# First cross-attention: the next unit's scores are moved ahead of this unit's transposes on TensorE, and its maxima ahead of the copies on VectorE

## The reference

```python
q = (x @ Wq).reshape(B, Nq, 16, 64)      # 112 rows
k = (context @ Wk).reshape(B, Nk, 16, 64)  # 375 rows
v = (context @ Wv).reshape(B, Nk, 16, 64)
scores = einsum('bqhd,bkhd->bhqk', q, k) / 8
attn = softmax(scores, axis=-1)
out = einsum('bhqk,bkhd->bqhd', attn, v).reshape(B, Nq, 1024) @ Wo + bo
x = layernorm(x + out)
```

## Time and profile before

| | |
|---|---|
| three timed runs | 1081.72 us median, 1080.94 to 1088.02 |
| the profiled execution | 1089.54 us, of which the span of instructions is 1087.7 us |
| TensorE busy | 1000.9 us, 92% |
| VectorE busy | 584.4 us, 54% |
| ScalarE busy | 411.1 us, 38% |
| mean granted TensorE clock | 0.964 of 2.4 GHz |
| first scores to last weigh of the first cross-attention | 143 to 465 us of the span |

### The profile page before, as it was taken

How to read it: one execution, slowest core, us unless ns; L and a number is a source line. 1 busy time by engine, 2 the same in 40 slices (tenths; PEclk the granted TensorE clock), 3 DMA queues, 4 the chain that set the end, 5 groups by cost and what they waited for, 6 DMA issues and landing times. The chain is left out here.

```text
span 1087.7 us, 17961 instructions
## 1 busy us (share of the span) xinstructions
PE 1000.9 (92%) x6656; PEld 775.4 (71%) x6656; DVE 584.4 (54%) x1316; ACT 411.1 (38%) x1068; POOL 150.5 (14%) x151
## 2 busy tenths in 40 slices
PE   6899799999999999969999996888889999999985
PEld 4587677877877877659999995565566767676653
DVE  1877545546555555646565554457524443544543
ACT  2555534333343343324545341366523222322221
POOL 0233410010110100004434342100010000000000
PEclk9999899999999999879999997999989999999996
DMA  4500000000000000046112000600000000001000
GB/s 147 187 2 1 30 15 2 15 15 2 14 0 0 0 0 0 1 171 191 40 39 77 0 2 29 136 2 2 2 18 15 15 15 15 15 1 27 5 5 13
DMA packets 24286, 34.34 MB, mean 32 GB/s; under 512 B 3168, under 2 KB 19888, under 8 KB 24224
## 3 DMA queue, kind: packets, MB, share of 16 engines
q1 hardware_dynamic: 24224, 33.51, 10.3%
HBM read 30.75 MB, written 2.75 MB: 31 GB/s over the span
## 5 line engine op out<-in xcount | busy, mean ns | idle before, releaser
L1041 ACT ACTIVATE x_prob<-bank,x_negmax 112x375 f32<-112x375 f32 x128 | 72.3, 570 | 154.7 <-DVE x_negmax L957 154.7
L1684 DVE TENSOR_TENSOR moe_h_low<-moe_sq,moe_h_high 128x448 fp32r<-128x448 f32 x64 | 54.7, 873 | 52.9 <-ACT moe_h_high L1749 39.6
L1725 POOL TENSOR_TENSOR moe_sq<-moe_r 128x448 f32<-128x448 f32 x64 | 64.1, 1004 | 122.8 <-ACT moe_r L1757 104.3
L88 PE MATMUL bank<-moe_w_low,moe_h_high 128*112 128x256 f32 x256 | 71.8, 280 | 0.0
L88 PE MATMUL bank<-moe_w_high,moe_h_high 128*112 128x256 f32 x256 | 71.7, 280 | 0.0
L88 PE MATMUL bank<-moe_w_high,moe_h_low 128*112 128x256 f32 x256 | 71.7, 280 | 0.0
L957 DVE TENSOR_REDUCE x_negmax<-bank 112x1 f32<-112x375 f32 x128 | 64.1, 543 | 8.4 <-PE bank L849 6.4
L1757 ACT ACTIVATE moe_r<-bank 128x448 f32<-128x448 f32 x64 | 34.9, 546 | 86.8 <-PE bank L88 85.1
L1436 ACT ACTIVATE x_prob<-bank,x_negmax 112x375 f32<-112x375 f32 x64 | 36.1, 569 | 75.9 <-DVE x_negmax L1306 75.9
L870 PEld LDWEIGHTS bank<-x_prob_t,x_v 125*64 125x64 f32 x768 | 38.1, 139 | 34.5 <-issue 30.5
L962 DVE COPY x_prob_t<-bank 125x336 f32<-125x336 f32 x128 | 58.9, 499 | 5.7 <-PE bank L858 3.7
(11 more groups left out here) (368 smaller groups left out, 2281.6 us busy)
## 6 DMA issues: line engine op xcount, KB each, us to landing
moe_w<-in_L_ffn_W SPq DMA_DIRECT2D x16, 512.0 KB, 4.6
ctx_t<-in_ctx_t SPq DMA_DIRECT2D x8, 376.0 KB, 4.4
x_ctx_t<-in_ctx_t SPq DMA_DIRECT2D x8, 376.0 KB, 3.3
wk<-in_L_xattn_Wk SPq DMA_DIRECT2D x2, 1024.0 KB, 6.9
wv<-in_L_xattn_Wv SPq DMA_DIRECT2D x2, 1024.0 KB, 9.7
wq<-in_L_xattn_Wq SPq DMA_DIRECT2D x2, 1024.0 KB, 11.8
wo<-in_L_xattn_Wo SPq DMA_DIRECT2D x2, 1024.0 KB, 13.3
w_in<-in_L_attn_W_in SPq DMA_DIRECT2D x1, 1160.0 KB, 7.2
```

The costliest lines, as they stand in the source:

```text
L88: last = pe.matmul(out, lhs, rhs, start=(k == 0), stop=(k == len(pairs) - 1))
L1041: act.activation(PROB(u, e)[:, :], S_BANK(u, e)[0:T, 0:S], ACT.Exp, bias=negmax[:, g:g + 1], accum_out=total[:, g:g + 1]).then_inc(p_ready, 1)
L1684: dve.tensor_tensor(h_low[half][:, m, :], sq[m % 2][:, :], h_high[half][:, m, :].bitcast(F32), ALU.subtract).then_inc(low_done, 1)
L1725: pool.tensor_tensor(sq[m % 2][:, :], r[m % 2][:, :], r[m % 2][:, :], ALU.mult).then_inc(sq_done, 1)
```

## The change

The code order of two calls is swapped on TensorE and on VectorE, and two waits are added. On TensorE a unit is now scores(u + 1), turn(u), weigh(u - 1), jobs. On VectorE it is row_max(u + 1), copy_turned(u), emptying. Each score now waits by itself for the exponential that reads its bank (`p_ready` of the same head of the unit before). Each exponential now waits until the transposes of the unit before have read its buffer (`pt_ready`), since they no longer stand ahead of the scores that it needs. No instruction is added or taken out but the waits, and the register arithmetic that they need in the loop.

```diff
@@ TensorE, scores
                     for e in range(PER):
                         rows = slice(e * DH, (e + 1) * DH)
+                        wait_past(pe, p_ready, (i * U + u - 1) * PER + e + 1)
                         last = pe.matmul(S_BANK(u, e)[0:T, 0:S], qt[p][rows, u, :], kt[p][rows, u, :], start=True, stop=True)
@@ TensorE, round_
                         if heads:
-                            turn(i, u)
                             if u + 1 < U:
                                 scores(i, u + 1, p)
                             elif front:
                                 scores(i + 1, 0, 1 - p)
+                            turn(i, u)
                             if u > 0:
                                 weigh(i, u - 1, p)
@@ VectorE, round_
                         if heads:
-                            copy_turned(i, u)
                             if u + 1 < U:
                                 row_max(i, u + 1)
                             elif front:
                                 row_max(i + 1, 0)
+                            copy_turned(i, u)
@@ ScalarE, exps
                         act.wait_ge(max_ready, (i * U + u) * PER + e + 1)
+                        wait_past(act, pt_ready, (i * U + u - 1) * PER + e + 1)
```

## The result

| | before | after |
|---|---|---|
| median of 12 runs | 1087.95 us (1080.94 to 1093.06) | 1096.11 us (1088.31 to 1097.29) |
| ratio | | 1.0071, 95% interval 1.0037 to 1.0104 |
| profiled execution, its span | 1089.54, 1087.7 us | 1088.31, 1086.5 us |

A forecast was written before the change was run, and what follows sets the result against it. TensorE, busy for 1000.9 of 1087.7 us, was taken as the bound. 10.6 us lost in busy units less 3.0 won in the last round gave +7.6, so 1089.3 us from 1081.72; range 1079.5 to 1095.5 us.

The forecast's parts named there:

- The price of a busy unit: TensorE in rounds 0 to 6: a fourth change of array shape adds 0.19 us a unit, +10.6 us over 56 units.
- the exit: TensorE going from a job's last product to the scores: 0.09 us more than the even spacing, in each busy unit.
- the bare load: Weight load of the first transpose after the scores, no longer hidden under a product: 0.10 us in each busy unit.
- the sum: Whole kernel: 10.6 us lost in 56 busy units less 3.0 us won in round 7, +7.6 us.
- The last round: Round 7, without jobs, where TensorE waits: 2.4 to 4.3 us won, taken as -3.0 us.
- the 0.84 us behind the output product: Round 7, unit 3: VectorE's copies no longer stand ahead of the maxima, so 0.84 us go.
- The cycle of 3.30 us: Round 7, units 1 and 4: transposes leave the chain between exponentials and scores, 2.79 us instead of 3.30.
- The two scores come apart: Rival on TensorE's score pair: the wait between them costs up to 0.4 us a unit, 22 us, together 1112 us; chance 0.10.
- the base: Time before the change to which the forecast was applied: 1081.72 us, the median of three runs.

The follow-up runs named there:

- The last-round version: The kernel before, with the new order in round 7 only and the old order without added waits in rounds 0 to 6; 1085.39 us median of 12, ratio 0.9988.
- the busy rounds alone: The kernel before, with the new order in rounds 0 to 6 only and round 7 in the old one; 1094.75 us median of 12, ratio 1.0071.

## Why the prediction was right about the change and wrong about the time

**The price of a busy unit** was right: 0.19 us forecast, 0.10 for the exit and 0.09 for the bare load measured. It stayed out of seven of the 56 units. Unit 0 of round 0 has no weigh and so no change of shape more (5.23 us in both). In the six others, unit 5 of rounds 1 to 6, the 5.16 us stay, for a wait absorbs the 0.19: the second job there waits for VectorE to empty the turned rows, and that wait, six times in rounds 1 to 6, went from 2.8 to 1.5 us in all (the rows of L88 above). I had said that TensorE is never idle in these rounds, from the busy share of the windows, and a busy share counts modelled ends. That makes 49 x 0.19 = 9.3 us (and 327.06 less 317.79) where the sum had 10.6.

**The last round** was right within its bounds of 2.4 and 4.3, and -3.0 a little short: 4.0 us against the trace shown, 2.5 against a trace in which the clock didn't fall there (320.33 less 317.79). One part of its working was wrong. I had taken the 0.84 us behind the output product as a gain of VectorE's swap in itself; alone that swap costs as much elsewhere. The cycle of 3.30 us came down to 2.93 in unit 4 (458.10 to 461.03, between starts of the first score) and to 2.38 in unit 1 (446.38 to 448.76), where I had 2.79 for both: behind a unit with a job the exponentials have a lead, and the unit is as short as TensorE's own work; the next one pays for part of it.

**The two scores come apart** only where I said it could be, in the last round, in four of its pairs. One of them:

```profile
448.76 1.29 PE L850 MATMUL bank<-x_kt,x_qt 64*112 64x375 f32 x4
448.91 0.20 ACT L1043 ACTIVATION_READ_ACCUMULATOR x_prob<-bank,x_negmax 112x1 f32 x1
...
449.97 0.73 PEld L859 LDWEIGHTS bank<-const,x_prob 112*125 112x125 f32 x6 [0.54 <-issue]
```

The pair lasts 1.21 instead of 0.81 us. That is the amount which the rival had named, but not its mechanism: the second score starts at 449.16, 0.05 after its exponential was read out (449.11), and so it is in all four pairs. It waits for the exponential, and nothing shows that the first score holds it back. In the busy units the pair keeps its 0.81.

**The rest of the 6.6 us of the stage** was in no term: 9.3 - 4.0 = 5.3, and 1.3 come behind the last weigh, where in this trace the output product met a stretch at 1.2 GHz (clock 0.84 over the 10.61 us). The last-round version, with the same round 7, keeps the full clock for 9.17 us behind its last weigh and ends its stage after 10.48. This is no accident of one trace: from the last weigh to the stage's end it takes 11.8 to 12.2 us, at a mean clock of 0.80 to 0.86, in all four traces whose rounds 0 to 6 have the change's order (both of the change, the busy rounds alone, TensorE's swap alone), and 10.3 to 10.5 us, at 0.91 to 1.00, in the six others. So some 1.5 us seem to come with the change itself; why the clock falls there was not tried and stays open.

**The step that failed** is the last one of the sum: "that one was 0.7% above the median of the three runs, 1081.72, so there I forecast 1089.3 us". I took two levels for scatter around one. The term that was wrong is the base: 1081.72 us, where the median of twelve is 1087.95. These 6.2 us are nearly all of the 6.8 by which 1089.3 missed 1096.11; the change itself was 0.6 off. The three runs shown, 1080.94, 1081.72 and 1088.02, and the profiled 1089.54 are two at each level. Against the execution that the sum was made from the forecast was 1097.1 us, and the upper level of the changed kernel is at 1096.98; against the lower one it was 1089.3, and that level is at 1089.18. Agreement to 0.1 us is luck, for terms of the sum were off by more and cancelled: 1.3 too much for the busy units, up to 1.0 too little for the last round, and 1.3 behind it that no term had. The traces differ by 6.3 us at the upper level and by 8.4 at the lower. The median of twelve fell into the upper group, seven to five. A range for a kernel whose few runs stand in two clumps 7 us apart has to reach from the lower clump plus the smallest effect to the upper one plus the largest: with the forecast's own +4 to +10.5 from 1085 to 1100 (1080.94 and 1089.54), and lower still for the rivals, but not ending at 1095.5.

**The rules.** That a change of tiling mode drains TensorE (the Trainium skill, "TensorEngine Tiling (Array Packing)", Key Properties) holds for the one pair that the trace of before lacked, from a job to half-row products: 0.10 us. What the array does in that time no trace shows. That weight loads are pulled ahead of running products (the Trainium skill, "TensorE: Matmul & The Clock Gate", Step-by-step) did not hold across a change of shape: in rounds 1 to 6 of all ten traces the first load of a new shape starts together with the first product of that shape (within 0.003 us), where the transposes' load behind a job started 0.09 to 0.23 us ahead.

## What to carry to other kernels

Count the changes of array shape in a loop of TensorE's work before reordering it: steps of the same shape belong side by side, and here each change more was 0.19 us, in 49 places, and nothing where a wait took it up. Where TensorE has no idle time, let a reordering run only where it waits, or choose an order that adds no change of shape: the last round alone, and scores, weigh, transposes, jobs in the busy rounds, both kept the last round's 25.0 us and the busy rounds' 41.3. When few runs stand in two clumps, give the time at each of them, and compare traces of the same clump, by stages, before reading any difference.

## What the runs showed that I had not expected

The level goes with the clock in unchanged stages: mean granted clock 0.973 in the runs of 1088.31 to 1089.20 us and 0.966 to 0.967 in those of 1096.03 to 1097.29, the same program each time. And two swaps on two engines, each harmful alone in the last round (30.30 and 31.84 us, where the old order takes 28.45 at the full clock), make 24.99 us together.
